# Residual stored early, normalized sums added to the output by accumulating transfers; a new order of the tail on VectorE and ScalarE

## The chip, the core and the metric

The kernel runs on one core of one Trainium2 chip. The metric is device microseconds of one execution, the median of the runs. Beside it stands one execution that the hardware profiler recorded. The core has five engines with a queue each: TensorE (PE), VectorE (DVE), ScalarE (ACT), GpSimd (POOL) and SyncE (SP). They wait for each other on semaphores, and 16 DMA engines carry all transfers.

## What is computed

A decoder layer on x, 4 batches of 512 tokens of 256 values, float32:

```python
x = x + _layernorm(attention(_layernorm(x)))
x = x + _layernorm(ffn(_layernorm(x)))

def ffn(x):                      # 2048 tokens
    routed = _moe_routed(x_flat, router, w_up_gate, w_down)     # 8 experts, the best 2 of each token, 640 slots each
    shared = _shared_mlp(x_flat, shared_w_up_gate, shared_w_down)   # silu(gate) * up, 704 wide, then down
    return (routed + shared).reshape(b, s, d)
```

The routed part copies each token into slots of its two experts, runs the experts on their slots, and takes for each token the weighted sum of its two results. The change concerns the last line, x + layernorm(routed + shared): x there is the residual after attention, which is complete long before the experts run.

## The kernel before

The work is written out by hand, engine by engine, in one block; every order and every wait is explicit. The 2048 tokens are 16 tiles of 128 tokens (`TILES`), four to a batch (`TPB`), and B = 4. `x_sb` holds the residual and `y_sb` the sum of the feed-forward part, 16 tiles of 128 x 256 each.

Attention comes first, 64 units of one head of one batch. Then half of the shared layer runs (`shared_up`, `shared_down` with j from 0 to 3, its hidden width being split in two parts), while GpSimd scatters the normalized tokens into the slots in DRAM. The eight experts follow, each with loads by SP (`load_slots`, `load_expert`, `load_down`) and a store of 640 rows of results to `yg_dram`. SP's queue handles its instructions in order, so a wait there holds all that is behind it.

Behind the experts is the tail. TensorE runs the second part of the shared layer, `shared_up` and `shared_down` with j from B to 2B - 1, one j for each batch. `shared_down(j)` leaves two halves of 2 tiles in PSUM; before it overwrites them it waits for VectorE's `shared_sum` of the batch before. ScalarE takes SiLU of the products (`silus`), VectorE multiplies (`shared_hidden`). GpSimd gathers the experts' rows back, 32 indirect transfers of 128 rows into 16 buffers (`got`, `GR` = 16), two for each tile; from the 17th on each waits until VectorE has used its buffer. VectorE adds them with their weights (`routed_sum(pair)`, two tiles, four instructions), adds the PSUM halves (`shared_sum`), and takes mean and variance (`piece_stats`). ScalarE takes the root, VectorE the inverse and the shift (`piece_scale`), ScalarE normalizes tile by tile (`out_normed`). The pieces are `LAST_LN`: batches 0, 1 and 2, and the two halves of batch 3.

In the kernel before, the residual is added behind that, by VectorE (`add_x`) for batches 0, 1 and 3 and by GpSimd for batch 2, and SP stores each piece to the output. VectorE's order is batch by batch: hidden products of the next batch, all four tiles' weighted sums, PSUM sums, statistics, scale, add; the weighted sums of batch 3 come ahead of the statistics of batch 2.

Of the kernel before, what the change touches and what calls it, by code (L numbers as in the profile page):

```python
# [11 lines left out]
ALU = mybir.AluOpType  # L12
# [26 lines left out]
def decoder_layer(nc, x, wq, w0, wout, cos_t, sin_t, ident, causal, before, iota8,  # L39
# [5 lines left out]
    B, SEQ, H, D, E, NE, NS, CAP, HID, SHID = dims  # L45
# [45 lines left out]
    with ExitStack() as ctx:  # L91
        def sem(name):
            return ctx.enter_context(nc.semaphore(name))
# [221 lines left out]
        yo_psum, yo_ready, yo_stored = sem("yo_psum"), sem("yo_ready"), sem("yo_stored")  # L315
        got_in = [sem(f"got_in{r}") for r in range(GR)]
        got_used = sem("got_used")
        out_ready = {"pool": sem("out_ready_pool"), "dve": sem("out_ready_dve")}
        stored = sem("stored")

        LAST_LN = [(b * TPB, (b + 1) * TPB) for b in range(B - 1)] + [(t, t + 2) for t in (TILES - 4, TILES - 2)]

# [118 lines left out]
        def _(sp):  # L441
# [87 lines left out]
            def load_slots(e, r):  # L529
                sp.dma_start(xg[:, r, :, :], xg_dram[bass.ds(e * CAP, CAP), :].rearrange("(p s) e -> p s e", p=P)) \  # L530
                    .then_inc(xg_in[r], 16)
# [7 lines left out]
            sp.wait_ge(scattered[ROUTED], 2 * (TILES - ROUTED * TPB) * 16)  # L539
            for e in range(2):  # L540
                load_slots(e, e)

            def expert_steps(e0, last):
                for r in range(2):
# [12 lines left out]
            with sp.Fori(0, NE // 2 - 1) as pair:  # L557
                expert_steps(pair * 2, False)
            expert_steps(NE - 2, True)
            for t0, t1 in LAST_LN:  # L560
                b = t0 // TPB
                if b == B - 2:
                    sp.wait_ge(out_ready["pool"], TPB)
                else:
                    sp.wait_ge(out_ready["dve"], t1 if b < B - 2 else t1 - TPB)
                sp.dma_start(out_v[b, :, t0 - b * TPB:t1 - b * TPB, :], y_sb[:, t0:t1, :]).then_inc(stored, 16)
            sp.wait_ge(stored, 16 * len(LAST_LN))

# [1 line left out]
        def _(act):  # L571
# [134 lines left out]
            def silus(j, tiles=range(SH)):  # L706
                for i in tiles:
                    w = SHW[j // B][i]
                    act.wait_ge(s_psum_g, sh_products(j, i, 1))
                    act.activation(s_sg[0:w, i, :], ps[2 * i][0:w, :], ACT.Silu).then_inc(s_silu, 1)  # L710
# [127 lines left out]
            for e in range(0, NE, 2):  # L838
                expert_steps(e, e == NE - 2)
            silus(B)  # L840
            for n, (t0, t1) in enumerate(LAST_LN):
                if n + 1 < B:
                    silus(B + n + 1)
                act.wait_ge(var2_ready, 2 * B + n + 1)
                act.activation(std[:, t0:t1], mv[:, t0:t1, 1], ACT.Sqrt, bias=eps_sb[:, 0:1]).then_inc(std2_ready, 1)
                act.wait_ge(shift_ready, B + n + 1)
                for t in range(t0, t1):
                    act.activation(y_sb[:, t, :], y_sb[:, t, :], ACT.Identity, scale=rstd[:, t:t + 1],
                                   bias=out_shift[:, t:t + 1]).then_inc(out_normed, 1)
# [380 lines left out]
        def _(dve):  # L1230
# [429 lines left out]
            for r in range(2):  # L1660
                dve.memset(s_hid[SHW[1][SH - 1]:, r, SH - 1, :], 0.0).then_inc(shared_padded, 1)

            def routed_sum(pair):
                for k in range(2):
                    for t in range(2 * pair, 2 * pair + 2):
                        g = 4 * pair + 2 * k + t % 2
                        dve.wait_ge(got_in[g % GR], 16 * (g // GR + 1))
                        if k == 1:
                            dve.wait_ge(got_used, g - 1)
                        dve.scalar_tensor_tensor(y_sb[:, t, :], got[:, g % GR, :], cw[:, k, t:t + 1], y_sb[:, t, :],  # L1670
                                                 ALU.mult, ALU.add).then_inc(got_used, 1)
                dve.wait_ge(got_used, 4 * (pair + 1))

            def piece_stats(n):
                t0, t1 = LAST_LN[n]
                dve.wait_ge(sy_taken, 2 * B + t1 // 2)
                tile_stats(t0, t1, lambda t: y_sb[:, t, :])
                mean_and_var(t0, t1).then_inc(var2_ready, 1)
# [5 lines left out]
                shift_of(ts, out_shift)  # L1684

            def add_x(t0, t1):
                for t in range(t0, t1):
                    dve.wait_ge(out_normed, t + 1)
                    dve.tensor_tensor(y_sb[:, t, :], x_sb[:, t, :], y_sb[:, t, :], ALU.add).then_inc(out_ready["dve"], 1)  # L1690

            shared_hidden(B)
            for b in range(B - 1):
                shared_hidden(B + b + 1)
                for half in range(2):
                    routed_sum(2 * b + half)
                shared_sum(B + b)
                if b == B - 2:
                    for half in range(2):
                        routed_sum(2 * (B - 1) + half)  # L1700
                piece_stats(b)
                piece_scale(b)
                if b < B - 2:
                    add_x(b * TPB, (b + 1) * TPB)
            for half in range(2):
                shared_sum(2 * B - 1, [half])
                piece_stats(B - 1 + half)
                piece_scale(B - 1 + half)
            add_x((B - 1) * TPB, TILES)

        @block.gpsimd
        def _(pool):
# [171 lines left out]
                    bounds_check=NE * CAP - 1, oob_is_err=False).then_inc(got_in[g % GR], 16)  # L1885

            for t in range((B - 2) * TPB, (B - 1) * TPB):
                pool.wait_ge(out_normed, t + 1)
                pool.tensor_tensor(y_sb[:, t, :], x_sb[:, t, :], y_sb[:, t, :], ALU.add).then_inc(out_ready["pool"], 1)  # L1890

# [71 lines left out]
```

## Time and profile before

| | us |
|---|---|
| median of 3 runs | 784.11 (783.74 to 785.61) |
| the profiled execution | 784.87 |
| its span, first to last instruction | 783.1 |
| TensorE busy | 737.4 (94%) |
| VectorE busy | 572.2 (73%) |
| GpSimd busy | 544.8 (70%) |
| ScalarE busy | 465.0 (59%) |

The execution is somewhat longer than the span, which leaves out what lies before the first and behind the last instruction. Busy shares are averages over stages with different limits. The tail behind the experts begins at about 720 us of the span.

### The profile page before, as it was taken

Reading aid. Unit: us, or ns where it says so; the run is one execution under the profiler, and the core shown is the slowest. Engines: PE = TensorE matmul, PEld = TensorE weight load, DVE = VectorE, ACT = ScalarE, POOL = GpSimd, SP = SyncE. Lnnn points to the kernel's source line nnn. Section 1 sums busy time; section 2 is a strip of 40 time slices with the busy share of each in tenths; the row PEclk is TensorE's granted clock in tenths of the full one; section 3 lists DMA queues with packets and bytes.
Section 4 is the critical chain, followed back from the end, with each engine's and each line's share of the span. In section 5 each row is a group of like instructions: output and inputs, shape, how many; then the busy total and the mean of one; then the engine's idle time right before and its main releaser. Section 6 shows DMA issues by size and latency. Waiting matters only on the chain.

```text
span 783.1 us, 13975 instructions
## 1 busy us (share of the span) xinstructions
PE 737.4 (94%) x4364; PEld 627.6 (80%) x4364; DVE 572.2 (73%) x1539; ACT 465.0 (59%) x1161; POOL 544.8 (70%) x459
## 2 busy tenths in 40 slices
PE   5799999999999999999999999999999999999992
PEld 4687788888888888888777888777778779998882
DVE  6977887677777776868888686888755337777577
ACT  5557777676667677665566676566543245554252
POOL 4467998787888877787888988788644054441773
PEclk9999999999999999999999999999999999999997
DMA  9411255422222222112122222212124043551352
GB/s 299 128 53 54 77 168 174 161 71 74 61 69 69 68 69 68 67 56 60 63 75 68 89 81 57 67 62 69 48 82 150 7 168 134 199 204 78 89 152 84
DMA packets 47749, 75.74 MB, mean 97 GB/s; under 512 B 9728, under 2 KB 24640, under 8 KB 47680
## 3 DMA queue, kind: packets, MB, share of 16 engines
q1 hardware_dynamic: 43504, 65.19, 26.2%
q0 software_dynamic: 3072, 8.39, 3.3%
q10 hardware_dynamic: 1104, 1.31, 0.5%
q8 instruction: 34, 0.56, 0.3%
q14 instruction: 35, 0.29, 0.1%
HBM read 57.71 MB, written 17.17 MB: 96 GB/s over the span
## 4 chain that ended last, share of the span: by engine, by line
PE 75%; DVE 10%; issue 7%; POOL 3%; ACT 3%; DMA 2%; DVEq 0%; ACTq 0%; POOLq 0%
PE ps L433 22%; PE ps L968 17%; PE ps L933 13%; PE ps L984 9%; PE ps L954 7%; PE ps L1132 3%; POOL got L1882 1%; DVE q_sw L1314 1%; DVE q_sw L1313 1%; POOL slot_inputs L1789 1%; POOL o_lo L1773 1%; PE ps L1167 1%; DMA kvh_rows<-hc_t 1%; PE ps L1194 1%; DVE stats L1253 1%
## 5 line engine op out<-in xcount | busy, mean ns | idle before, releaser
L968 PE MATMUL ps<-pt,vp 128*128 128x512 f32 (+3 forms) x512 | 149.5, 434 | 10.3 <-DVE q_sw L1314 10.0
L634 ACT ACTIVATE prob<-ps,neg_max 128x512 f32<-128x512 f32 (+3 forms) x256 | 132.6, 525 | 33.4 <-DVE neg_max L1323 30.6
L968 PEld LDWEIGHTS ps<-pt,vp 128*128 128x128 f32 x512 | 82.7, 190 | 59.9 <-issue 30.5
L1754 POOL TENSOR_TENSOR q_sw<-q_cos,q_sw 128x512 f32<-128x512 f32 x62 | 79.2, 1277 | 65.5 <-DVE q_cos L1315 65.4
L1323 DVE CUSTOM_DVE_ANT_0 ps<-ps,causal_row 128x512 f32<-128x512 f32 (+3 forms) x256 | 120.1, 511 | 4.6 <-PE ps L933 4.5
L643 ACT ACTIVATE pt<-ps,vcol 128x512 f32<-128x512 f32 x64 | 44.2, 690 | 109.4 <-PE ps L954 109.4
L1773 POOL TENSOR_TENSOR o_lo<-o_t,o_hi 128x512 fp32r<-128x512 f32 x64 | 84.2, 1316 | 33.4 <-ACT o_hi L672 33.4
L954 PE MATMUL ps<-id_f,prob 128*128 128x128 f32 x640 | 92.3, 275 | 0.9 <-ACT pt L643 0.9
L933 PE MATMUL ps<-k_hi,q_hi 128*128 128x512 f32 x248 | 86.6, 349 | 0.4 <-POOL q_lo L1758 0.3
L1342 DVE TENSOR_TENSOR o_t<-ps,inv_row 128x512 f32<-128x512 f32 x64 | 44.3, 692 | 52.5 <-PE ps L968 52.5
L1758 POOL TENSOR_TENSOR q_lo<-q_sw,q_hi 128x512 fp32r<-128x512 f32 x62 | 80.1, 1292 | 2.6 <-ACT q_hi L666 2.3
L1763 POOL TENSOR_TENSOR k_lo<-kh_row,k_hi 128x512 fp32r<-128x512 f32 x62 | 79.0, 1274 | 1.9 <-ACT k_hi L660 1.9
L954 PEld LDWEIGHTS ps<-id_f,prob 128*128 128x128 f32 x640 | 72.5, 140 | 9.5 <-issue 1.3
L933 PE MATMUL ps<-k_lo,q_hi 128*128 128x512 f32 x248 | 80.1, 323 | 0.0
L933 PE MATMUL ps<-k_hi,q_lo 128*128 128x512 f32 x248 | 80.0, 323 | 0.0
L1313 DVE TENSOR_TENSOR q_sw<-ps,rope_sb 64x512 f32<-64x512 f32 x64 | 44.4, 693 | 48.3 <-PE ps L433 46.3
L1768 POOL TENSOR_TENSOR kh_row<-kt,kh_row 128x512 f32<-128x512 f32 x62 | 79.6, 1284 | 0.0
L1789 POOL DMA_INDIRECT slot_inputs<-xn,at_in x32 | 33.5, 1046 | 34.4 <-DVE at_in L1477 27.5
L433 PE MATMUL ps<-xt_hi,wq_hi 128*128 128x512 f32 x128 | 51.5, 402 | 4.0 <-DVE q_sw L1314 3.0
L672 ACT CAST o_hi<-o_t 128x512 fp32r<-128x512 f32 x64 | 39.8, 622 | 25.6 <-DVE o_t L1342 25.6
L652 ACT ACTIVATE pt<-ps,vcol 128x384 f32<-128x384 f32 (+1 forms) x128 | 53.3, 473 | 0.0
L984 PE MATMUL ps<-wo_hi,o_hi 128*128 128x256 f32 x256 | 52.6, 327 | 0.0
(220 smaller groups left out, 1935.6 us busy)
## 6 DMA issues: line engine op xcount, KB each, us to landing
kh_row<-kvh_rows SPq DMA_DIRECT2D x64, 256.0 KB, 3.2
inv_row<-inverse_sums SPq DMA_DIRECT2D x64, 256.0 KB, 3.1
slot_inputs<-zeros SPq DMA_DIRECT2D x8, 640.0 KB, 4.8
xg<-slot_inputs SPq DMA_DIRECT2D x8, 640.0 KB, 4.7
slot_outputs<-yo SPq DMA_DIRECT2D x8, 640.0 KB, 3.3
up_raw<-in_w_up_dram SPq DMA_DIRECT2D x8, 368.0 KB, 4.8
wo_raw<-in_wout_dram SPq DMA_DIRECT2D x4, 512.0 KB, 8.0
dn_sb<-in_w_dn_dram SPq DMA_DIRECT2D x8, 256.0 KB, 3.7
```

The lines of the kernel that those rows point to most:

```text
L433: last = pe.matmul(psum, w(o), m(o), start=(o == 0 and j == 0), stop=(o == EO - 1 and j == 2))
L634: ins = act.activation(prob[:, i % 2, ROW_AT[nt]:ROW_AT[nt] + w], ps_s[bank][:, at:at + w], ACT.Exp, scale=-1.0, bias=neg_max[:, i % 2, nt ...
L933: ins = pe.matmul(ps_s[bank][:, at:at + w], q_[:, r, qs], k_[:, r, 0:w], start=(nt == tiles[0] and j == 0), stop=(nt == tiles[-1] and j == ...
L954: ins = pe.transpose(ps_pt[bank][:, dst:dst + P], prob[:, i % 2, src:src + P], id_f[:])
L968: ins = pe.matmul(ps_qo[:, mt * P:SEQ], vp[:, b * TPB + mt, :], pt[:, i % 2, cols], start=(mt == 0), stop=(mt == PT_BANKS[-1][-1]))
L984: ins = pe.matmul(ps_acc[t // 2][:, at:at + E], o_[:, r, t * P:(t + 1) * P], w[:, h, :], start=(h == 0 and j == 0 and t % 2 == 0), stop=(h ...
L1323: ins = dve.tensor_tensor_reduce(s_, s_, causal_row[:, (NT - 1 - nt) * P:], 1.0, BIG, ALU.add, ALU.min, neg_max[:, i % 2, nt:nt + 1])
L1754: pool.tensor_tensor(q_sw[:], q_cos[:], q_sw[:], ALU.add).then_inc(q_sum_ready, 1)
L1758: pool.tensor_tensor(q_lo[:, i % 2, :], q_sw[:], q_hi[:, i % 2, :].bitcast(F32), ALU.subtract) \
L1763: pool.tensor_tensor(k_lo[:, i % 2, :], kh_row[:, i % 2, :], k_hi[:, i % 2, :].bitcast(F32), ALU.subtract) \
L1768: pool.tensor_tensor(kh_row[:, i % 2, :], kt[:, tok(batch(i))], kh_row[:, i % 2, :], ALU.mult) \
L1773: pool.tensor_tensor(o_lo[:, i % 2, :], o_t[:], o_hi[:, i % 2, :].bitcast(F32), ALU.subtract) \
```

## The change

Four things. SP stores the residual, `x_sb`, to the output as soon as the first two experts' rows are asked for, in four transfers of 512 KB. Behind the experts nothing is added by VectorE or GpSimd; instead GpSimd, behind its last gather, issues five transfers that add the normalized pieces to the output in DRAM (`accum_op`). VectorE's tail is written out in a new order, two tiles at a time, in which the weighted sums come as their gathers land, and the scale of a piece comes after later sums. ScalarE takes SiLU of one batch more ahead of the first root.

```diff
--- before.py
+++ after.py
@@ -315,8 +315,7 @@
         yo_psum, yo_ready, yo_stored = sem("yo_psum"), sem("yo_ready"), sem("yo_stored")
         got_in = [sem(f"got_in{r}") for r in range(GR)]
         got_used = sem("got_used")
-        out_ready = {"pool": sem("out_ready_pool"), "dve": sem("out_ready_dve")}
-        stored = sem("stored")
+        stored, x2_stored = sem("stored"), sem("x2_stored")
 
         LAST_LN = [(b * TPB, (b + 1) * TPB) for b in range(B - 1)] + [(t, t + 2) for t in (TILES - 4, TILES - 2)]
 
@@ -539,6 +538,9 @@
             sp.wait_ge(scattered[ROUTED], 2 * (TILES - ROUTED * TPB) * 16)
             for e in range(2):
                 load_slots(e, e)
+            sp.wait_ge(x2_ready, 2 * B - 1)
+            for b in range(B):
+                sp.dma_start(out_v[b], x_sb[:, b * TPB:(b + 1) * TPB, :]).then_inc(x2_stored, 16)
 
             def expert_steps(e0, last):
                 for r in range(2):
@@ -557,13 +559,7 @@
             with sp.Fori(0, NE // 2 - 1) as pair:
                 expert_steps(pair * 2, False)
             expert_steps(NE - 2, True)
-            for t0, t1 in LAST_LN:
-                b = t0 // TPB
-                if b == B - 2:
-                    sp.wait_ge(out_ready["pool"], TPB)
-                else:
-                    sp.wait_ge(out_ready["dve"], t1 if b < B - 2 else t1 - TPB)
-                sp.dma_start(out_v[b, :, t0 - b * TPB:t1 - b * TPB, :], y_sb[:, t0:t1, :]).then_inc(stored, 16)
+            sp.wait_ge(x2_stored, 16 * B)
             sp.wait_ge(stored, 16 * len(LAST_LN))
 
 
@@ -838,9 +834,10 @@
             for e in range(0, NE, 2):
                 expert_steps(e, e == NE - 2)
             silus(B)
+            silus(B + 1)
             for n, (t0, t1) in enumerate(LAST_LN):
-                if n + 1 < B:
-                    silus(B + n + 1)
+                if n + 2 < B:
+                    silus(B + n + 2)
                 act.wait_ge(var2_ready, 2 * B + n + 1)
                 act.activation(std[:, t0:t1], mv[:, t0:t1, 1], ACT.Sqrt, bias=eps_sb[:, 0:1]).then_inc(std2_ready, 1)
                 act.wait_ge(shift_ready, B + n + 1)
@@ -1660,7 +1657,9 @@
             for r in range(2):
                 dve.memset(s_hid[SHW[1][SH - 1]:, r, SH - 1, :], 0.0).then_inc(shared_padded, 1)
 
-            def routed_sum(pair):
+            def routed_sum(pair, after_shared=False):
+                if after_shared:
+                    dve.wait_ge(sy_taken, 2 * B + pair + 1)
                 for k in range(2):
                     for t in range(2 * pair, 2 * pair + 2):
                         g = 4 * pair + 2 * k + t % 2
@@ -1684,29 +1683,34 @@
                 shift_of(ts, out_shift)
 
 
-            def add_x(t0, t1):
-                for t in range(t0, t1):
-                    dve.wait_ge(out_normed, t + 1)
-                    dve.tensor_tensor(y_sb[:, t, :], x_sb[:, t, :], y_sb[:, t, :], ALU.add).then_inc(out_ready["dve"], 1)
-
             shared_hidden(B)
-            for b in range(B - 1):
-                shared_hidden(B + b + 1)
-                for half in range(2):
-                    routed_sum(2 * b + half)
-                shared_sum(B + b)
-                if b == B - 2:
-                    for half in range(2):
-                        routed_sum(2 * (B - 1) + half)
-                piece_stats(b)
-                piece_scale(b)
-                if b < B - 2:
-                    add_x(b * TPB, (b + 1) * TPB)
-            for half in range(2):
-                shared_sum(2 * B - 1, [half])
-                piece_stats(B - 1 + half)
-                piece_scale(B - 1 + half)
-            add_x((B - 1) * TPB, TILES)
+            shared_hidden(B + 1, [0])
+            routed_sum(0)
+            shared_hidden(B + 1, [1, 2])
+            routed_sum(1)
+            shared_sum(B)
+            piece_stats(0)
+            routed_sum(2)
+            shared_hidden(B + 2)
+            routed_sum(3)
+            piece_scale(0)
+            shared_sum(B + 1)
+            piece_stats(1)
+            routed_sum(4)
+            shared_hidden(B + 3)
+            routed_sum(5)
+            piece_scale(1)
+            shared_sum(B + 2)
+            piece_stats(2)
+            routed_sum(6)
+            piece_scale(2)
+            shared_sum(2 * B - 1, [0])
+            piece_stats(B - 1)
+            shared_sum(2 * B - 1, [1])
+            piece_scale(B - 1)
+            routed_sum(7, True)
+            piece_stats(B)
+            piece_scale(B)
 
 
         @block.gpsimd
@@ -1885,9 +1889,12 @@
                     bounds_check=NE * CAP - 1, oob_is_err=False).then_inc(got_in[g % GR], 16)
 
 
-            for t in range((B - 2) * TPB, (B - 1) * TPB):
-                pool.wait_ge(out_normed, t + 1)
-                pool.tensor_tensor(y_sb[:, t, :], x_sb[:, t, :], y_sb[:, t, :], ALU.add).then_inc(out_ready["pool"], 1)
+            pool.wait_ge(x2_stored, 16 * B)
+            for t0, t1 in LAST_LN:
+                b = t0 // TPB
+                pool.wait_ge(out_normed, t1)
+                pool.dma_start(out_v[b, :, t0 - b * TPB:t1 - b * TPB, :], y_sb[:, t0:t1, :],
+                               accum_op=ALU.add).then_inc(stored, 16)
 
 
 # ---- launch: one core; inputs and outputs as the reference has them ----
```

## Rows read from the trace of the kernel before

**Rows 1.** The page: its heading, and the chain that ended last, by engine.
```profile
span 783.1 us, 13975 instructions
...
PE 75%; DVE 10%; issue 7%; POOL 3%; ACT 3%; DMA 2%; DVEq 0%; ACTq 0%; POOLq 0%
```
**Rows 2.** The chain in order of time (start us, us, what), third expert and tail.
```profile
662.46 0.89 PE ps L433 x6
...
767.46 3.12 DMA got<-slot_outputs,at_out
770.60 0.50 DVE y_sb L1670
...
780.05 0.42 DVE y_sb L1690
```
**Rows 3.** Timeline, GpSimd's tail (start, us, engine, line, operation, count, [idle before]).
```profile
724.36 1.09 POOL L1882 DMA_INDIRECT got<-slot_outputs,at_out  x1 [8.66 <-DMA slot_outputs<-yo]
...
767.46 1.28 POOL L1882 DMA_INDIRECT got<-slot_outputs,at_out  x1 [0.30 <-issue]
774.40 2.77 POOL L1890 TENSOR_TENSOR y_sb<-x_sb,y_sb 128x256 f32<-128x256 f32 x4 [5.66 <-ACT y_sb L848]
```
**Rows 4.** Timeline, VectorE's tail.
```profile
748.70 3.37 DVE L1670 SCALAR_TENSOR_TENSOR y_sb<-got,cw,y_sb 128x256 f32<-128x256 f32 x8
...
753.43 1.41 DVE L1364 BATCH_NORM_STATS2 stats<-y_sb 128x6 f32<-128x256 f32 x4
754.87 0.38 DVE L1369 BATCH_NORM_AGGREGATE mv<-stats 128x2 f32<-128x6 f32 x4
755.62 0.18 DVE L1683 RECIPROCAL rstd<-std 128x4 f32<-128x4 f32 x1 [0.36 <-ACT std L845]
755.83 0.16 DVE L1392 SCALAR_TENSOR_TENSOR out_shift<-mv,rstd 128x4 f32<-128x4 f32 x1
...
773.60 0.68 DVE L1579 TENSOR_TENSOR y_sb<-ps,y_sb 128x512 f32<-128x512 f32 x1
774.32 0.75 DVE L1364 BATCH_NORM_STATS2 stats<-y_sb 128x6 f32<-128x256 f32 x2
775.10 0.25 DVE L1369 BATCH_NORM_AGGREGATE mv<-stats 128x2 f32<-128x6 f32 x2
```
**Rows 5.** Timeline, TensorE at the first expert and in the tail.
```profile
639.88 1.06 PE L1167 MATMUL ps<-id_f,xg 128*128 128x128 f32 x8
...
757.98 5.34 PE L1132 MATMUL ps<-sdn_sb,s_hid 128*128 128x256 f32 x24
766.22 5.42 PE L1132 MATMUL ps<-sdn_sb,s_hid 128*128 128x256 f32 x24 [2.90 <-DVE y_sb L1579]
```
**Rows 6.** Timeline, ScalarE's last root and normalizations.
```profile
778.21 0.29 ACT L845 ACTIVATE std<-mv,eps_sb 128x2 f32<-128x2 f32 x1 [0.58 <-DVE mv L1369]
778.93 1.09 ACT L848 ACTIVATE y_sb<-y_sb,out_shift,rstd 128x256 f32<-128x256 f32 x2 [0.43 <-DVE out_shift L1392]
```
**Rows 7.** DMA issues from 700 us on: KB each, median us from issue to landing.
```profile
got<-slot_outputs,at_out POOLq DMA_INDIRECT x32, 3.0
out_dram<-y_sb SPq DMA_DIRECT2D x2, 256.0 KB, 2.2
```
**Rows 8.** Stretches: us, busy time of each engine, TensorE clock, DMA share, GB/s.
```profile
760.00:761.00 1.00, 1.00 (x7) 0.87 (x6) 0.95 (x2) 0.98 (x4) 0.91 (x1) 1.00 1.08 385
...
770.00:778.00 8.00, 1.64 (x8) 1.11 (x6) 6.10 (x22) 3.65 (x8) 2.77 (x4) 0.80 0.00 2
...
778.00:783.00 5.00, 0.00 (x0) 0.00 (x0) 2.02 (x8) 1.39 (x3) 0.00 (x0) 0.50 0.63 210
```
**Rows 9.** Timeline, SP's issues at the kernel's start and ahead of the experts.
```profile
9.55 5.10 SPq L456 DMA_DIRECT2D wo_raw<-in_wout_dram  x4
...
635.64 6.08 SPq L530 DMA_DIRECT2D xg<-slot_inputs  x3
```
**Rows 10.** The tile of expert rows between 635 and 642 us, issue to landing.
```profile
DMA to landing us min/median/max: 4.0/4.1/5.3
```

## Prediction

> **What bounds the kernel now.** I read the page's chain of waits first [rows 1]. TensorE carries three quarters of the 783.1 us span, but the change touches nothing of it ahead of the tail, so the chain in order of time is read next, for the end alone [rows 2]. There it stands on GpSimd's gathers and no longer on TensorE. The last gather is issued at 767.46 and its rows are there at 770.60. From then on VectorE and ScalarE alternate in a fixed order, and the last add stands at 780.05 and is over at 780.47. Its 256 KB store takes 2.2 us to land [rows 7], 782.7, and 0.4 us go by until the span ends. GpSimd's timeline [rows 3] shows 32 gathers, evenly spaced: (767.46 - 724.36) / 31 = 1.39 us each. They don't depend on the tail's order while the buffers come free in time. VectorE's timeline [rows 4] shows why 10 us lie behind the last gather: the last two batches' eight-instruction weighted sums, sums from PSUM, statistics and scales are all done late, and TensorE's last products even wait 2.90 us for VectorE [rows 5].
>
> So two things set the end: the work on VectorE and ScalarE behind TensorE's last products, and whatever carries the result out. The change shortens the first and replaces the second.
>
> **Part 1, the new order on VectorE and ScalarE.** Eight sums of a batch take 3.37 us, so four take 1.7. A half sum from PSUM is 0.68, statistics of four tiles 1.41 + 0.38, of two tiles 0.75 + 0.25, a scale 0.18 + 0.16 and about 0.04 of gaps, 0.38 [rows 4]. I lay the new order against TensorE, whose products for batch 2 end at 757.98 + 5.34 = 763.3 [rows 5]. Is VectorE up to date by then? Gather 23 is issued at about 724.36 + 23 x 1.39 = 756.3 and lands 3.0 later [rows 3, 7], 759.3. The last hidden product of batch 3 is finished close to that, since TensorE's products for it end at 758.0. Four sums, a scale and a half sum (1.7 + 0.4 + 0.7) then bring VectorE to about 762.3, before TensorE is done. TensorE needs this last half sum to go on, so its wait of 2.90 us is gone and its last products end near 768.3.
>
> From 763.4 VectorE's list is: half sum 0.7, statistics of four 1.8, four sums 1.7, scale 0.4, half sum 0.7, statistics of two 1.0, half sum 0.7, scale 0.4 (770.8 so far), four sums 1.7, statistics of two 1.0. That is 10.1 us, with gaps 10.4, so 773.8. The last four sums start at 770.8, just behind the last gather's landing at 770.6, so nothing waits there. A root of 0.29, a scale of 0.38 and two normalizations of 1.09 [rows 6] put the last normalized tile at about 775.7. Before, it was 780.02 (778.93 + 1.09). The add of 0.42 behind it goes too. Worth of this part: 4.3 + 0.4 = 4.7 us up to the moment at which the last store can be issued.
>
> ScalarE's SiLU now runs one batch ahead of the roots, so there are fewer changes of its table; I cost this at nothing, since it waits for TensorE in that stretch anyway. GpSimd's four adds (2.77 us, [rows 3]) stand beside ScalarE's and are off the chain. The gathers' pace doesn't change: the 16 buffers are taken a second time from gather 16 on, and the last four of them, issued from 762 on, reuse what batch 1's sums freed by 748.70 + 3.37 = 752.1 [rows 4]; the new order does these sums no later.
>
> **Part 2, the residual stored early.** Four issues on SP's queue follow the first two loads of expert rows, which start at 635.64 [rows 9]; the load behind them waits for TensorE and is issued by 641.3 at the earliest. Four issues of 512 KB took 5.10 us where the transfers were backed up [rows 9], so SP is free again by about 636.4 + 5.1 = 641.5: at most 0.2 us late. The rows that follow are the third expert's, which starts at 662.46 [rows 2]; 2 MB ahead of them in the queue cost some 6 us (below) of the 20 that there are. So nothing there. One thing is tight: TensorE takes the first expert's rows at 639.88 [rows 5], when they have only just landed (4.0 to 4.1 us behind 635.64, [rows 9, 10]). If the stores behind them slow them, every later step moves. From below this costs 0; from above 1.3 us, since the slowest landing of the three loads was 5.3 [rows 10]. I take 0, as the stores stand behind in the same queue, and keep 1.3 for a rival.
>
> **Part 3, the accumulating transfers.** All of the result, 2 MB in five pieces, now leaves from GpSimd's queue, behind its last gather. The first piece, long normalized, is issued at 768.74 + 0.30 = 769.0 [rows 3]; the two last ones stand behind the pieces ahead of them, on GpSimd and in the DMA engines. The trace has no accumulating transfer and no plain GpSimd store, so it is bounded.
>
> Transfer time: the last three stores before, 1 MB, took 0.63 x 5 us = 3.15 us of all 16 engines' time, so 2 MB are 6.3 us; at the peak of 385 GB/s [rows 8] they are 5.4. From below an accumulating row costs no more than a stored one. From above it costs twice as much, because two rows are read, the normalized one and the residual in the output, for one that is written. I take twice: loads, stores and gathers here all move at a similar rate whichever side DRAM is on, so the count of rows passed should matter. That gives 10.9 to 12.6 us, and I take the middle, 11.7.
>
> When do they end? A 128-row gather lands 3.0 us behind its issue [rows 7], of which 0.4 us is its own transfer (6.3 / 16). The stream that begins at 769.0 therefore ends at 769.0 + 2.6 + its transfer time. At 11.7 us: 783.3, plus the 0.4 behind the last landing, 783.7. VectorE's chain alone would need 775.8 + 2.6 + 0.8 + 0.4 = 779.6. The later of the two counts, so **the stream of accumulating transfers sets the end** and eats what part 1 gains: 783.7 against 783.1, 0.6 us more.
>
> The Trainium skill ("Collectives: The Full Stack", section on the bandwidth ceiling and why AG, RS and AR differ) says that a reduce in the DMA engines emits two read descriptors for each written chunk and that its measured rate is 1/1.93 of the copy's. No row here shows it; by that factor the stream would be 10.4 to 12.2 us.
>
> GpSimd's own time: a gather of 128 rows occupies it for 1.01 us [rows 3]. A piece has 512 or 256 rows. From below its cost is that of a gather, 1.0 us, whatever the rows, and then all five are issued in time. From above it grows with the rows, 4.0 and 2.0 us. 
>
> **The sum.** Last normalization 4.3 us earlier, last add 0.4 less, store replaced by a stream that ends at 783.3 instead of 782.7: +0.6 us. The profiled execution took 784.87, 1.77 more than its span, and lies 0.76 above the median of 784.11. Applied to the median, 784.11 + 0.6 is 784.7; I say 784.8.
>
> **Rivals.**
> A, accumulation is hidden: a row costs less than about 1.2 times a stored one, so that the stream (7.6 us or less) ends before VectorE's chain does. Then the span ends at 779.6, 3.5 us less, 780.6 for the median. For it: the 16 engines moved next to nothing from 770 to 778 [rows 8], so nothing stands in the stream's way, and the last piece is small. Against it: two reads per row. The gain stays over 0.3% up to a factor of 1.4.
> B, slower by GpSimd: issue time grows with rows. Pieces of 4.0, 4.0, 4.0, 2.0 with 0.30 between put the last issue at 769.0 + 15.2 = 784.2, which lands 4.4 us later: 788.6, with the 0.4 a span of 789.0, 5.9 us more, 790.0. It decides from 3.5 x + 1.2 = 10.3, that is from x = 2.6 us for 512 rows: above that GpSimd alone makes the kernel slower than before.
> C, the early stores hold up the first expert: 1.3 us on top of the forecast, 786.1. For it: the landing has 0.2 us to spare. Against it: they queue behind.
> D, the order doesn't do what it says: some sum waits for gathers or SiLU, so that normalization is late. It would be hidden by the stream unless it costs over 4 us, and I find no such wait; part of the other cases' width.
>
> **How the numbers follow.** Forecast (two reads per row, stream-bound) 0.42; its own range is 782.7 to 786.9, as single-rate times of 5.4 to 6.3 and factors of 1.8 to 2.2 allow. A 0.32, B 0.18, C 0.08. The measurement tells about 0.3%, 2.35 us, from no change. Faster by over that: A, and the best of the forecast's factors, 0.33. Slower: B, the half of C that passes the bound, and the forecast's worst factors (from 13.4 us of transfer), 0.31. Within: 0.36. The range goes from A with a slightly shorter gather chain, 779.8, to B, 790.0.
>
> **What would show it.** Right: the last normalization ends near 775.7 and TensorE's 2.9 us wait is gone (part 1); TensorE still turns the first expert's rows at about 639.9 (part 2); behind the last gather the DMA engines are busy without a break from 770.6 until just before the end, and each 512 KB accumulation takes about twice the time that a store's bytes took (part 3). Wrong: DMA engines idle between the last pieces (A), GpSimd's issues several us long and back to back (B), TensorE waiting at 640 (C), or VectorE waiting for gathers in the last 15 us (D).

## The result, and the profile after

| | kernel before | changed kernel |
|---|---|---|
| median of 20 runs, side by side (us) | 784.95 (783.74 to 787.77) | 786.7 (784.57 to 789.86) |
| the profiled execution | 784.87 | 786.55 |
| its span | 783.1 | 784.8 |
| VectorE busy | 572.2 (73%) | 565.7 (72%) |
| GpSimd busy | 544.8 (70%) | 547.6 (70%) |

The ratio of the changed kernel to the one before is 1.0025, 95% interval 1.0016 to 1.0035: about 2 us slower. The interval does not reach 1, but the difference is smaller than the 0.3% that the prediction took as the least that can be told. The forecast was +0.6 us.

Part 1 did its work. The changed kernel's timelines of TensorE, VectorE and ScalarE, in that order (columns as in [rows 3]), are the counterparts of [rows 4 to 6]:

```profile
757.05 10.52 PE L1129 MATMUL ps<-sdn_sb,s_hid 128*128 128x256 f32 x48
...
769.56 1.67 DVE L1669 SCALAR_TENSOR_TENSOR y_sb<-got,cw,y_sb 128x256 f32<-128x256 f32 x4
771.26 0.75 DVE L1361 BATCH_NORM_STATS2 stats<-y_sb 128x6 f32<-128x256 f32 x2
...
773.06 1.09 ACT L845 ACTIVATE y_sb<-y_sb,out_shift,rstd 128x256 f32<-128x256 f32 x2 [0.43 <-DVE out_shift L1389]
```

TensorE's 48 last products run in one piece, without the 2.90 us wait, and the last tile is normalized at 773.06 + 1.09 = 774.15, where it was 780.02. But the result still has to leave. GpSimd's timeline and the two groups of DMA issues (KB each, median us from issue to landing) are the counterparts of [rows 3, 7]:

```profile
765.48 1.15 POOL L1886 DMA_INDIRECT got<-slot_outputs,at_out  x1 [0.31 <-issue]
766.63 4.14 POOL L1896 DMA_DIRECT2D out_dram<-y_sb  x3
771.05 1.19 POOL L1896 DMA_DIRECT2D out_dram<-y_sb  x1 [0.28 <-ACT y_sb L845]
774.44 1.20 POOL L1896 DMA_DIRECT2D out_dram<-y_sb  x1 [2.21 <-ACT y_sb L845]
```
```profile
out_dram<-y_sb POOLq DMA_DIRECT2D x3, 512.0 KB, 8.8
out_dram<-y_sb POOLq DMA_DIRECT2D x2, 256.0 KB, 8.2
```

The stretches (columns as in [rows 8]) show one unbroken stream from about 768.6 to 780.4, as estimated from the first and last stretch with traffic. It moves at 135 to 200 GB/s; 200 is about half of the 385 GB/s of [rows 8]:

```profile
770.00:771.00 1.00, 0.00 (x0) 0.00 (x0) 1.00 (x4) 0.75 (x2) 0.77 (x1) 1.00 1.18 175
...
776.00:777.00 1.00, 0.00 (x0) 0.00 (x0) 0.00 (x0) 0.00 (x0) 0.00 (x0) 0.50 1.24 200
...
780.00:781.00 1.00, 0.00 (x0) 0.00 (x0) 0.00 (x0) 0.00 (x0) 0.00 (x0) 0.50 0.44 68
781.00:782.00 1.00, 0.00 (x0) 0.00 (x0) 0.00 (x0) 0.00 (x0) 0.00 (x0) 0.50 0.02 3
782.00:783.00 1.00, 0.00 (x0) 0.00 (x0) 0.00 (x0) 0.00 (x0) 0.00 (x0) 0.50 0.00 0
```

At 782 all is at rest, and yet the span goes on to 784.8. What goes on is found in the instructions of line 91, the end of the block, where each engine's sequencer closes. Columns: line, sequencer, operation, count, duration in ns (min/median/max), start of the first and last. First the kernel before, whose rows I had not read, then the changed kernel:

```profile
L91 POOLq DRAIN  x1: 6653/6653/6653, 775.8 to 775.8; - x1
...
L91 SPq COMPARE_BRANCH  x1: 38/38/38, 782.7 to 782.7; - x1
```
```profile
L91 POOLq DRAIN  x1: 10101/10101/10101, 774.4 to 774.4; - x1
L91 SPq COMPARE_BRANCH  x1: 38/38/38, 781.7 to 781.7; - x1
...
L91 SPq EVENT_SEMAPHORE  x1: 17/17/17, 784.7 to 784.7; - x1
```

SP's COMPARE_BRANCH stands right behind its wait for the stores, so I read it as the moment at which SP has seen all transfers landed: 782.7 before, 781.7 now, one microsecond earlier. GpSimd's closing DRAIN ended at 775.8 + 6.65 = 782.4 before, just ahead of that moment, and ends at 774.4 + 10.1 = 784.5 now, 2.8 us behind it. SP, which had closed 0.3 us behind its COMPARE_BRANCH before, now closes at 784.7, right behind GpSimd's drain, and the other engines' last rows stand there too. I read this as a wait for the last of them.

The whole part ahead of the tail differs between executions (the first gather is issued at 724.36 before and at 723.44 after, and in the runs below between 723.8 and 727.9). Positions in the tail are therefore compared from the first gather on. The table holds them for all runs of this case; the experiments below are read with it. Each entry is a row's start plus its duration less the first gather's start; for SP it is the start of its COMPARE_BRANCH.

| us behind the first gather | gathers issued | last tile normalized | GpSimd's last work done | SP sees all landed | GpSimd's drain over | end of span |
|---|---|---|---|---|---|---|
| before | 44.4 | 55.7 | 52.8 | 58.3 | 58.1 | 58.7 |
| changed | 43.2 | 50.7 | 52.2 | 58.3 | 61.1 | 61.4 |
| order_alone | 43.2 | 52.9 | 49.3 | 55.5 | 54.6 | 55.9 |
| accum_old_order | 44.4 | 55.5 | 57.0 | 61.0 | 63.8 | 64.0 |
| plain_gpsimd_store | 43.2 | 50.7 | 51.7 | 53.6 | 57.5 | 57.7 |
| early_store_alone | 44.4 | 55.6 | 52.7 | 58.2 | 58.1 | 58.6 |
| hybrid | 44.5 | 50.7 | 47.3 | 55.1 | 56.5 | 56.7 |
| first_piece_early | 45.4 | 50.7 | 52.2 | 57.3 | 60.1 | 60.3 |
| late_gpsimd_memset | 43.2 | 52.9 | 53.5 | 55.6 | 58.8 | 59.1 |
| order_fewer_gpsimd_adds | 43.2 | 51.6 | 46.2 | 55.7 | 51.5 | 56.0 |
| gpsimd_waits_landing | 43.2 | 50.7 | 52.2 | 57.4 | 63.4 | 63.5 |

Each row is one execution. What the engines set alone repeats closely: the last tile is normalized at 50.7 in all five kernels with the new order and no GpSimd adds. The landing of the accumulating stream doesn't: gpsimd_waits_landing does the same work as the changed kernel up to there and has it 0.8 us sooner (57.4 against 58.3). A difference of under 1 us between two such landings therefore says little.

So the question for the chip: is it the transfer's double cost that ate the gain of part 1, as forecast, or the closing of GpSimd, which the forecast did not have, and what makes that long?

### The profile page after: what moved, and what is told of

It reads as the page before. It is cut to its first block, busy times and chain, and to the rows that moved or that the text cites. A ratio compares the mean times of both kernels' runs of the same rounds, so it can differ in the third digit from the quotient of the medians.

```text
span 784.8 us, 13961 instructions
## 1 busy us (share of the span) xinstructions
PE 736.5 (94%) x4364; PEld 627.5 (80%) x4364; DVE 565.7 (72%) x1527; ACT 463.0 (59%) x1159; POOL 547.6 (70%) x460
## 4 chain that ended last, share of the span: by engine, by line
PE 75%; DVE 8%; issue 6%; POOL 4%; ACT 3%; DMA 2%; POOLq 0%; DVEq 0%; ACTq 0%; SPq 0%
PE ps L432 23%; PE ps L965 16%; PE ps L930 13%; PE ps L981 9%; PE ps L951 7%; PE ps L1129 2%; POOL got L1886 2%; POOL slot_inputs L1793 1%; PE ps L1164 1%; DVE q_sw L1311 1%; DVE q_sw L1310 1%; POOL out_dram L1896 1%; POOL o_lo L1777 1%; DMA kvh_rows<-hc_t 1%; PE ps L1191 1%
## 5 line engine op out<-in xcount | busy, mean ns | idle before, releaser
L1310 DVE TENSOR_TENSOR q_sw<-ps,rope_sb 64x512 f32<-64x512 f32 x64 | 44.4, 693 | 48.3 <-PE ps L432 46.4
L432 PE MATMUL ps<-xt_hi,wq_hi 128*128 128x512 f32 x128 | 51.6, 403 | 4.0 <-DVE q_sw L1311 3.0
```

Source lines behind the costliest of these rows:

```text
L432: last = pe.matmul(psum, w(o), m(o), start=(o == 0 and j == 0), stop=(o == EO - 1 and j == 2))
```

## The experiments

**The order alone.** The changed kernel without the early stores and without accumulation; the residual is added by VectorE for batches 0 and 3 and by GpSimd for 1 and 2, and SP stores the pieces.

```diff
-            for b in range(B):
-                sp.dma_start(out_v[b], x_sb[:, b * TPB:(b + 1) * TPB, :]).then_inc(x2_stored, 16)
...
-            shared_hidden(B + 3)
+            shared_hidden(B + 3, [0])
+            add_x(0, 2)
+            shared_hidden(B + 3, [1])
+            add_x(2, TPB)
+            shared_hidden(B + 3, [2])
...
             piece_scale(B)
+            add_x(3 * TPB, TILES)
...
-                pool.dma_start(out_v[b, :, t0 - b * TPB:t1 - b * TPB, :], y_sb[:, t0:t1, :],
-                               accum_op=ALU.add).then_inc(stored, 16)
+            for t in range(TPB, 3 * TPB):
+                pool.wait_ge(out_normed, t + 1)
+                pool.tensor_tensor(y_sb[:, t, :], x_sb[:, t, :], y_sb[:, t, :], ALU.add).then_inc(out_ready["pool"], 1)
```

> The new order of VectorE and ScalarE alone: no early store, no accumulation; the residual is added by VectorE (batches 0 and 3) and GpSimd (batches 1 and 2) and SP stores the pieces. Theory (the order is worth 4.7 us up to the last store's issue, and the changed kernel loses it in the accumulating stream and in what follows it): the last add is over near 775, span 777.5 to 779.5, ratio to the kernel before 0.993 to 0.995. Rival 1 (the order is worth nothing once stores and adds are back): ratio 0.999 to 1.001. Rival 2 (GpSimd's closing drain takes about 5.3 us behind its last instruction, whatever that is, and bounds the end): with the last GpSimd add near 773 it ends near 778, and the span with it, ratio 0.994. The drain's start and end in the trace tell these apart.

Measured: 781.58 us (779.97 to 785.02), ratio 0.9965 (0.9951 to 0.9979), faster than both kernels. GpSimd's drain is over 0.9 us before the last landing, so it costs nothing. The gain is 2.8 us of the tail, not the 4.7 of part 1, and the ratio lies outside the 0.993 to 0.995 that were expected. Its timelines of GpSimd and VectorE say why:

```profile
767.19 6.09 POOL L1908 TENSOR_TENSOR y_sb<-x_sb,y_sb 128x256 f32<-128x256 f32 x8
```
```profile
765.45 2.11 DVE L1673 SCALAR_TENSOR_TENSOR y_sb<-got,cw,y_sb 128x256 f32<-128x256 f32 x4
...
770.82 3.15 DVE L1673 SCALAR_TENSOR_TENSOR y_sb<-got,cw,y_sb 128x256 f32<-128x256 f32 x4
```

The same four weighted sums take 1.67 us in the changed kernel. Here GpSimd's adds run from 767.19 to 773.28, and the sums beside them take up to 3.15. The last normalized tile comes at 52.9 instead of 50.7.

**Stores and accumulation with the old order.** The kernel before, its adds removed, with the early stores and the five accumulating transfers.

```diff
+            for b in range(B):
+                sp.dma_start(out_v[b], x_sb[:, b * TPB:(b + 1) * TPB, :]).then_inc(x2_stored, 16)
...
-            add_x((B - 1) * TPB, TILES)
...
-                pool.tensor_tensor(y_sb[:, t, :], x_sb[:, t, :], y_sb[:, t, :], ALU.add).then_inc(out_ready["pool"], 1)
+            pool.wait_ge(x2_stored, 16 * B)
+            for t0, t1 in LAST_LN:
+                b = t0 // TPB
+                pool.wait_ge(out_normed, t1)
+                pool.dma_start(out_v[b, :, t0 - b * TPB:t1 - b * TPB, :], y_sb[:, t0:t1, :],
+                               accum_op=ALU.add).then_inc(stored, 16)
```

> Early stores and accumulating transfers with the order of the kernel before on VectorE and ScalarE. Theory: the last normalization stays near 780, the last accumulation is issued there and lands 4 to 6 us later, and GpSimd's drain follows by 2.9 us: span 787 to 790, ratio 1.005 to 1.009. Rival (the stream sets the end whatever the order, as it begins behind the last gather): the same end as the changed kernel, ratio 1.002 to 1.003.

Measured: 790.03 us, ratio 1.0064 (1.0039 to 1.0088). The pieces now come late (the last tile at 55.5), so all is landed at 61.0 only, 2.7 us later than in the kernel before; another 2.8 us of drain follow. The two halves of the change thus pull against each other: the order is worth about 2.8 us of tail without accumulation and 2.6 us with it, and accumulating instead of adding and storing costs 5.3 to 5.5 in either order, the drain included (64.0 against 58.7, 61.4 against 55.9).

**Plain stores in place of accumulating ones.** This kernel leaves the residual out of the output: its last transfers overwrite it.

```diff
-                pool.dma_start(out_v[b, :, t0 - b * TPB:t1 - b * TPB, :], y_sb[:, t0:t1, :],
-                               accum_op=ALU.add).then_inc(stored, 16)
+                pool.dma_start(out_v[b, :, t0 - b * TPB:t1 - b * TPB, :], y_sb[:, t0:t1, :]).then_inc(stored, 16)
```

> The changed kernel with the five last transfers as plain GpSimd stores: the residual is then missing from the output. Theory (accumulation costs two reads per row): 2 MB move in 6 to 6.5 us instead of 11.8, each 512 KB lands within 5 us, the last piece lands near 778, and the span ends near 781, ratio 0.995 to 0.998. Rival (the path by GpSimd costs the time, not the addition): the transfers take over 10 us as in the changed kernel, ratio 1.001 to 1.004.

Measured: 783.63 us, ratio 0.9990 (0.9973 to 1.0008). Its stretches, DMA issues and line 91:

```profile
772.00:773.00 1.00, 0.00 (x0) 0.00 (x0) 0.90 (x4) 0.89 (x3) 0.00 (x0) 1.00 1.03 352
...
777.00:778.00 1.00, 0.00 (x0) 0.00 (x0) 0.00 (x0) 0.81 (x2) 0.00 (x0) 0.50 0.36 131
778.00:779.00 1.00, 0.00 (x0) 0.00 (x0) 0.00 (x0) 0.00 (x0) 0.71 (x1) 0.50 0.00 0
```
```profile
out_dram<-y_sb POOLq DMA_DIRECT2D x3, 512.0 KB, 4.3
out_dram<-y_sb POOLq DMA_DIRECT2D x2, 256.0 KB, 3.0
```
```profile
L91 POOLq DRAIN  x1: 6453/6453/6453, 778.1 to 778.1; - x1
L91 SPq COMPARE_BRANCH  x1: 38/38/38, 780.7 to 780.7; - x1
```

The same rows as plain stores move at up to 352 GB/s against 200, a factor of 1.76, and here the DMA engines are idle before the last piece. All is landed at 53.6 instead of 58.3: the accumulation itself costs 4.7 us. But the span is shorter by only 3.7 us, because GpSimd's drain ends 3.9 us behind the last landing. Without any accumulation the drain is still what ends last. It is not the accumulation alone that makes it long.

The edit changes one thing more, the size of the packets. The DMA packets from 700 us on, first of the kernel before and the changed kernel (the same line in both), then of this one:

```profile
DMA packets 4246, 8.60 MB, mean 86 GB/s; under 512 B 656, under 2 KB 2704, under 8 KB 4240
DMA packets 2894, 9.10 MB, mean 91 GB/s; under 512 B 688, under 2 KB 688, under 8 KB 2888
```

The 2 MB of output leave in 2704 - 656 = 2048 packets of 1 KB when GpSimd accumulates them, and in larger ones when GpSimd only stores them. But the kernel before, where SP stores the same rows, has the same 2048 packets, and they cost no more than the larger ones. The share of DMA time over the rate gives the time of all 16 engines for a MB: 0.63 / 0.210 = 3.0 us there (778 to 783 in [rows 8]) and 1.03 / 0.352 = 2.9 here (772 to 773), against 1.24 / 0.200 = 6.2 in the changed kernel (776 to 777). So the packets' size isn't what slows the stream. The adding takes 2.1 times the DMA time of storing the same rows; that this is because two rows are read for one written, no run shows.

**The early stores alone.** The kernel before with the four stores of the residual; its own stores overwrite them.

```diff
             for e in range(2):
                 load_slots(e, e)
+            sp.wait_ge(x2_ready, 2 * B - 1)
+            for b in range(B):
+                sp.dma_start(out_v[b], x_sb[:, b * TPB:(b + 1) * TPB, :]).then_inc(x2_stored, 16)
...
+            sp.wait_ge(x2_stored, 16 * B)
```

> The kernel before with the four early stores of the residual added; the end is as before and overwrites them. Theory: TensorE takes the first expert's rows 0.2 to 0.4 us later and nothing else moves: ratio 1.000 to 1.001. Rival (the early stores hold up the experts' loads and are what the changed kernel loses): over 1.3 us, ratio 1.002 or more.

Measured: 784.83 us, ratio 1.0008 (0.9993 to 1.0023). The tail is that of the kernel before (58.6 against 58.7). TensorE waits 0.38 us for the first expert's rows, 0.24 in the changed kernel. Part 2 costs no more than that wait, and the ratio's interval includes 1.

**A late memset on GpSimd.** The order alone, with one column of zeros written by GpSimd behind VectorE's last add: 0.1 us of work that nothing uses.

```diff
+            pool.wait_ge(out_ready["dve"], 2 * TPB)
+            pool.memset(zeros[:, 0:1], 0.0)
```

> The new order alone (adds by VectorE and GpSimd, SP stores) with one more GpSimd instruction at its very end: a memset of one column that waits for VectorE's last add. Theory (GpSimd's closing drain ends about 5.3 us behind its last instruction of any kind): the memset ends near 777.5, the drain near 782.8, the span 3 us longer than without it, ratio to before 0.999 to 1.001. Rival (the drain is long only where GpSimd's transfers are in flight): the drain ends within 2 us and the span stays at that of the order alone, ratio 0.995 to 0.998.

Measured: 785.4 us, ratio 1.0009 (0.9997 to 1.0022), where the order alone had 0.9965. GpSimd's timeline and line 91:

```profile
768.85 6.08 POOL L1908 TENSOR_TENSOR y_sb<-x_sb,y_sb 128x256 f32<-128x256 f32 x8
779.05 0.10 POOL L1910 MEMSET zeros<- 128x1 f32 x1 [4.12 <-DVE y_sb L1693]
```
```profile
L91 POOLq DRAIN  x1: 5417/5417/5417, 779.0 to 779.0; - x1
L91 SPq COMPARE_BRANCH  x1: 38/38/38, 781.2 to 781.2; - x1
```

The transfers land as in the order alone (55.6 against 55.5), and the span is 3.1 us longer, because the drain ends 5.3 us behind the memset, long after SP's stores have landed. This shows most plainly that the drain alone can set the end: the last transfers here are SP's, and GpSimd's gathers are long over.

**GpSimd waits for its own transfers.** The changed kernel with one wait more.

```diff
                                accum_op=ALU.add).then_inc(stored, 16)
+            pool.wait_ge(stored, 16 * len(LAST_LN))
```

> The changed kernel, with one wait more: behind its five accumulating transfers GpSimd waits until all of them have landed, and only then enters its closing drain. Nothing of the work changes. So far the drain ended at the later of two points, some 5.3 us behind GpSimd's last instruction and some 2.8 us behind the landing of its last accumulating transfer. Three readings. (1) The drain itself takes about 5.3 us from the moment at which GpSimd has nothing else to do, a wait included: it begins at the landing, 58.3 us behind the first gather, and ends at 63.6 instead of 61.1; the span is 2.5 us longer than that of the changed kernel, ratio to the kernel before 1.005 to 1.007. (2) It is tied to the landing alone: 2.8 us behind it as before, ratio 1.001 to 1.004, the same as the changed kernel. (3) What took the 2.8 us was the drain finding transfers still on their way; with all landed it is short, below 1 us, and the span ends at about 59, 2 us less, ratio 0.998 to 1.001.

Measured: 790.85 us, ratio 1.0084 (1.0054 to 1.0113). Line 91:

```profile
L91 POOLq COMPARE_BRANCH  x1: 46/46/46, 781.5 to 781.5; - x1
L91 SPq COMPARE_BRANCH  x1: 38/38/38, 781.5 to 781.5; - x1
L91 POOLq DRAIN  x1: 5706/5706/5706, 781.7 to 781.7; - x1
```

The drain begins when all has landed and still takes 5.7 us. The tail is 63.5, against 61.4 of the changed kernel. So the first reading holds: the drain takes 5 to 6 us from the moment GpSimd has nothing else to do, a wait included (forecast to end at 63.6, it ends at 63.4; the ratio's point lies somewhat above the 1.007 of the text, its interval takes it in). That the end fits so well is partly chance: the landing came 0.9 us sooner than the forecast took it, and the end of the drain stands 5.9 us behind it instead of 5.3. The drain doesn't consist of waiting for transfers. That in the changed kernel part of it runs beside the transfers, so that only 2.8 us of it stand behind them, fits this and isn't shown by itself.

**The first piece earlier.** The changed kernel with its first accumulating transfer issued between gathers 23 and 24.

```diff
             for g in range(2 * TILES):
                 k, t = g // 2 % 2, g // 4 * 2 + g % 2
+                if g == 24:
+                    pool.wait_ge(x2_stored, 16 * B)
+                    add_piece(0)
...
+            for n in range(1, len(LAST_LN)):
+                add_piece(n)
```

> The changed kernel with one edit: the first accumulating transfer is issued between gathers 23 and 24. Theory (the stream behind the last gather sets the end at about 5.7 us per MB): the stream is 1.5 MB, 2.9 us shorter, but the gathers end 1.7 us later by GpSimd's own time, so the end is about 1.2 us earlier than the changed kernel's: ratio to before 1.000 to 1.002. Rival (only the last piece and what follows it set the end): no gain on the changed kernel, ratio 1.002 to 1.004.

Measured: 785.92 us, ratio 1.0020 (1.0005 to 1.0035). All is landed 1.0 us earlier (57.3), the gathers are issued 2.2 us later, and the span's tail is 1.1 us shorter (60.3). The earlier landing is hardly more than two executions of the same stream differ by, and the ratio can't be told from the changed kernel's 1.0025. The drain again ends 2.8 us behind the landing.

**A hybrid.** The new order; batches 0 to 2 accumulated, the first of them between the gathers; batch 3 added by VectorE and stored by SP.

```diff
+            for t0, t1 in LAST_LN[B - 1:]:
+                b = t0 // TPB
+                sp.wait_ge(out_ready, t1 - b * TPB)
+                sp.dma_start(out_v[b, :, t0 - b * TPB:t1 - b * TPB, :], y_sb[:, t0:t1, :]).then_inc(last_stored, 16)
...
+            for t in range((B - 1) * TPB, TILES):
+                dve.wait_ge(out_normed, t + 1)
+                dve.tensor_tensor(y_sb[:, t, :], x_sb[:, t, :], y_sb[:, t, :], ALU.add).then_inc(out_ready, 1)
```

> The new order; batches 0 to 2 are stored early and accumulated by GpSimd, batch 0 between gathers 23 and 24 instead of behind the last one; batch 3 is added by VectorE and stored by SP. Theory (the end is the later of the accumulating stream's landing plus about 2.9 us of GpSimd's drain, and the last SP store): 1 MB of accumulation behind the last gather lands 8 to 9 us behind its issue, the drain ends near 778, the last store lands near 777, span 777 to 779, ratio 0.991 to 0.995, below the new order alone. Rival (early accumulation holds up the gathers behind it in the same queue): the last gathers land 2 to 3 us later, VectorE waits for them, ratio 0.996 to 0.999.

Measured: 784.03 us, ratio 0.9983 (0.9968 to 0.9998): a small gain, short of what was expected and of the order alone. Its DMA issues and line 91:

```profile
out_dram<-y_sb POOLq DMA_DIRECT2D x3, 512.0 KB, 6.6
out_dram<-y_sb SPq DMA_DIRECT2D x2, 256.0 KB, 3.9
```
```profile
L91 POOLq DRAIN  x1: 10608/10608/10608, 773.8 to 773.8; - x1
L91 SPq COMPARE_BRANCH  x1: 37/37/37, 783.0 to 783.0; - x1
```

The two accumulations behind the gathers and SP's last stores are under way together: the stores land in 3.9 us instead of 2.2, at 55.1, and the drain lasts until 56.5, 1.4 us behind them. What was expected of the drain held: its last accumulation is issued at 773.8 and lands 7.8 us later, at 781.6, and the drain ends 2.8 us behind that, at 784.4. The times ahead of it missed. The gathers are issued at 44.5 instead of 43.2, the accumulation behind them lands 9.2 us behind its first issue, beside SP's stores, and those land late. The ratio lies in the rival's range, but not for the rival's reason: the gathers are 1.3 us late and not 2 to 3, and VectorE isn't held up, for the last tile is normalized at 50.7 as in the changed kernel. By the point values, less accumulation is better and none is best; the intervals of the hybrid and of the order alone overlap.

**Fewer adds on GpSimd.** The order alone, with batch 2's adds on VectorE at the end.

```diff
             piece_stats(B)
+            add_x(2 * TPB, 2 * TPB + 2)
             piece_scale(B)
-            add_x(3 * TPB, TILES)
+            add_x(2 * TPB + 2, TILES)
...
-            for t in range(TPB, 3 * TPB):
+            for t in range(TPB, 2 * TPB):
```

> The new order alone, with batch 2's residual added by VectorE instead of GpSimd (GpSimd keeps batch 1's). Theory (in the order-alone kernel GpSimd's adds slowed VectorE's last four weighted sums from 1.67 to 3.15 us): the sums are back at 1.7 us, the last add ends about 1.2 us earlier, span 778 to 779.5, ratio 0.993 to 0.996, below the order alone. Rival (the four more adds on VectorE cost what the contention did): ratio as the order alone, 0.996 to 0.998.

Measured: 782.24 us, ratio 0.9967 (0.9955 to 0.9980), as the order alone, and as the rival of the text had it. Its VectorE timeline:

```profile
774.45 1.67 DVE L1673 SCALAR_TENSOR_TENSOR y_sb<-got,cw,y_sb 128x256 f32<-128x256 f32 x4
...
778.02 2.09 DVE L1693 TENSOR_TENSOR y_sb<-x_sb,y_sb 128x256 f32<-128x256 f32 x6
```

The sums are back at 1.67 us and the last tile is normalized 1.3 us earlier, but four more adds stand on VectorE, and the last pieces, with batch 2's store just ahead of them, land in 3.1 us instead of 2.2. It comes out even (56.0 against 55.9).

## Why the prediction was right and where it was not

The kind of bound was right: the stream of accumulating transfers lands last, long behind the normalization, and takes what the new order gains. That the kernel came out slower is in part luck. The forecast's +0.6 us was a stream that lands 0.6 us later than the last store before. From the first gather on it lands where that store landed, 58.3 in both, so by the prediction's own mechanism the two kernels would have come out even. All of the slowdown stands behind the landing, in GpSimd's drain, which the prediction doesn't have. The size was off by 1.4 us (2 us measured, 0.6 forecast), and two errors of opposite sign stand behind that.

- **Part 1.** Forecast: last normalization 4.3 us earlier. Measured from the first gather: 50.7 against 55.7, 5.0 us. TensorE's 2.90 us wait is gone, as said.
- **The gathers' pace.** The prediction took it as unchanged. It isn't: the gathers are all issued 1.2 us sooner in every kernel with the new order and no piece between them (43.2 against 44.4). The stream starts 43.2 behind the first gather, not at 769.0 - 724.36 = 44.6. This is 1.4 us to the good. No gather waited for a buffer: GpSimd is idle for 0.30 to 0.31 us between any two of them in either kernel. The gathers themselves are shorter, 33.7 us in sum instead of 34.9. The longest one before and the same one now:

```profile
762.71 1.82 POOL L1882 DMA_INDIRECT got<-slot_outputs,at_out  x1 [0.30 <-issue]
761.53 1.01 POOL L1886 DMA_INDIRECT got<-slot_outputs,at_out  x1 [0.30 <-issue]
```

  Before, VectorE ran its eight weighted sums beside this gather (761.98 to 765.35); whether that lengthened it wasn't tested.
- **Part 2.** Forecast: nothing, with TensorE at 639.9. The changed kernel's timeline has the first rows at 640.09, and SP is free for its next load at 641.58, where the forecast had it at 641.5:

```profile
640.09 1.06 PE L1164 MATMUL ps<-id_f,xg 128*128 128x128 f32 x8 [0.24 <-DMA xg<-slot_inputs]
...
636.56 3.48 SPq L543 DMA_DIRECT2D out_dram<-x_sb  x4
641.58 0.92 SPq L529 DMA_DIRECT2D xg<-slot_inputs  x1
```

  Rival C is out, by early_store_alone as well.
- **Part 3, the transfer.** Forecast: 11.7 us of transfer, by two rows read for one written. Measured: about 768.6 to 780.4, 11.8 us; the factor in DMA time is 2.1. That it came so near to 11.7 is partly chance: the forecast's own bounds were 10.9 and 12.6, and the same stream landed 0.8 us sooner in gpsimd_waits_landing. From the first issue to the last landing it is 781.7 - 766.6 = 15.1 us instead of the forecast's 14.3. Rival A, accumulation at less than 1.2 times the cost of a store, is out by plain_gpsimd_store: 352 against 200 GB/s. The factor between reduce and copy that the Trainium skill gives ("Collectives: The Full Stack", section on the bandwidth ceiling), 1.93, is near the 1.76 of these rows.
- **Part 3, GpSimd's issues.** 4.14 us for three issues of 512 rows together, 1.38 each on average, and 1.20 for one of 256, below the 2.6 at which rival B would have decided. (With the 4.4 us to landing that rival B itself uses, the limit is (783.3 - 769.0 - 4.4 - 1.2) / 3.5 = 2.5; that changes nothing.) The lower end of that bound was the nearer one. The Trainium skill's remark that descriptor generation is small ("DMA: Bandwidth & Descriptors", section on the anatomy of a GpSimd transfer) agrees with that as far as these rows go.
- **Behind the landing.** This is the step that failed. The prediction carried over 0.4 us from the last landing to the end of the span. Measured: 3.1 us. The 0.4 of the kernel before was the closing of SP behind its own store, and it held because GpSimd had been done with its last instruction 5.5 us earlier (52.8 against 58.3). GpSimd's drain ended 0.25 us ahead of the landing even then: the next thing to be late already stood there, in rows that the prediction didn't read. Giving GpSimd the last transfers moved its drain onto the path. The chain of the kernel before couldn't show this: it gives GpSimd's sequencer 0% [rows 1], since SP's own wait ended last, by that quarter of a microsecond.

From the first gather on: the landing came 0.7 us earlier than forecast (1.4 earlier start, 0.8 longer from first issue to last landing), and what follows it 2.7 us later, so the tail was 2.0 us longer than forecast, 2.6 us longer than before. That the spans differ by 1.7 and not by 2.6 us is the part ahead of the tail, 0.9 us shorter in that execution; the ratio of the runs, 2 us, lies between.

Could the 2.8 us behind the landing be the accumulation's own completion, and not the drain? late_gpsimd_memset and gpsimd_waits_landing speak against it: in the first, 0.1 us of memset with no transfer of GpSimd's under way costs 3.1 us, and in the second the drain takes 5.7 us although everything has landed. Both show a long drain without such a transfer under way. They don't show that transfers under way add nothing to it, and in the changed kernel it ends 8.9 us behind GpSimd's last issue.

What stays open: what the drain does in its 5 to 6 us, and why it ends 2.8 us behind the landing of the last accumulation in each of the four kernels where that is still under way when the drain begins (changed, accum_old_order, first_piece_early: 2.80, 2.76, 2.81; hybrid: 2.8). All accumulations here are issued by GpSimd, so nothing parts them from its drain but the wait of gpsimd_waits_landing.

## What to carry to other kernels

Before the last work of a kernel is moved to another engine, read how that engine closes: the instructions at the end of the block have a price per engine, here at most 0.4 us on SP and over 5 us on GpSimd, and it is hidden only as long as the engine stops early. Take the early stores and the accumulation out of this change and keep the order: 0.9965 of the time before, against 1.0025 with them. An addition that an engine does beside other work for 0.42 us a tile wasn't worth replacing by a transfer that moves every byte at little over half the rate (200 against 352 GB/s). Letting a quarter of the bytes leave early didn't change that here (first_piece_early, 1.0020).

## What was not expected of the hardware

- GpSimd's closing drain takes 5.3 to 5.7 us behind its last instruction (kernel before 5.3, plain stores 5.7, memset 5.3, wait for landing 5.7 from the drain's own start), longer when accumulating transfers are under way (8.9 us in the changed kernel). VectorE's took 0.2 to 0.9 us and ScalarE's 1.1.
- Four weighted sums on VectorE took 1.67 us alone and 3.15 us beside GpSimd's adds, in the same order of work.
- A 512 KB accumulation landed in 8.8 us in the stream, the same bytes stored by GpSimd in 4.3, by SP in 3.1.
